# FFN chunks of a post-norm layer: z ahead of the transposes of h1, the second silu ahead of the norm's products, the centring behind the second norm's product

## What is computed

```python
# _L0_attn_ref: 12 layers of attention without a softmax, all linear in x but for q.k.v
for i in range(12):
    q, k, v = split(x @ Wqkv[i].T + bqkv[i])          # 16 heads of 8 channels
    att = einsum('bhqd,bhkd->bhqk', q, k) * scale
    y = einsum('bhqk,bhkd->bhqd', att, v)
    x = y @ Wproj[i].T + bproj[i] + x
x = layernorm(x_in + attention(x_in))                  # h1 below
gate, up = h1 @ w_gate.T / 127, h1 @ w_up.T / 127      # 384 hidden channels
x = layernorm(h1 + (silu(gate) * up) @ w_down.T / 127)
```

## Time and profile before

| what | us |
|---|---|
| median of 3 runs (lowest, highest) | 336.1 (335.86, 336.31) |
| the profiled execution, in all | 335.32 |
| its span | 333.5 |
| granted clock of PE over the span | 0.999 |
| PE busy | 317.8 (95% of the span) |
| DVE busy | 226.4 (68%) |
| ACT busy | 183.0 (55%) |
| POOL busy | 96.6 (29%) |

### The profile page before, as it was taken

One profiled execution on the slowest core, in us unless ns is written; L12 is line 12 of the kernel. 1 busy time (PEld: TensorE's weight loads), 2 busy tenths in 40 slices (PEclk: granted clock), 3 DMA queues, 4 the chain that ended last, 5 costly groups with the idle time before them and its releaser, 6 DMA issues.

```text
span 333.5 us, 8348 instructions
## 1 busy us (share of the span) xinstructions
PE 317.8 (95%) x3336; PEld 288.9 (87%) x3336; DVE 226.4 (68%) x638; ACT 183.0 (55%) x417; POOL 96.6 (29%) x89
## 2 busy tenths in 40 slices
PE   8899999999999999999999999999999999999993
PEld 7879889798897998979979799797997988888873
DVE  1167676775775757757677576676765569998974
ACT  3338757376483774846738467385572164444550
POOL 2006046050320502305023050140505034555533
PEclk9999999999999999999999999999999999999999
DMA  8751001010010200102002010020000000111112
GB/s 232 267 220 61 4 2 61 2 63 2 2 61 3 63 0 3 63 0 63 2 2 62 2 52 12 2 62 2 2 3 2 0 1 0 31 48 46 33 34 67
DMA packets 10660, 13.66 MB, mean 41 GB/s; under 512 B 512, under 2 KB 8832, under 8 KB 10496
## 3 DMA queue, kind: packets, MB, share of 16 engines
q1 hardware_dynamic: 8368, 11.94, 11.4%
q10 hardware_dynamic: 2256, 1.21, 1.3%
HBM read 11.04 MB, written 2.10 MB: 39 GB/s over the span
## 4 chain that ended last, share of the span: by engine, by line
PE 80%; DVE 9%; issue 3%; DMA 3%; ACT 2%; POOL 1%; ACTq 0%; POOLq 0%; DVEq 0%
PE ps L797 14%; PE ps L850 13%; PE ps L885 13%; PE ps L748 6%; PE ps L746 6%; PE ps L747 6%; PE ps L964 3%; PE ps L806 3%; PE ps L836 3%; DMA xt<-x_tok 3%; DVE s_rows L581 3%; PE ps L813 2%; DVE xt L681 2%; DVE mt L574 2%; PE ps L953 1%
## 5 line engine op out<-in xcount | busy, mean ns | idle before, releaser
L346 POOL TENSOR_TENSOR step_lo<-step,step_hi 128x512 fp32r<-128x512 f32 x44 | 54.9, 1279 | 180.3 <-ACT step_hi L430 180.3
L746 PE MATMUL ps<-state_hi,step_hi 128*128 128x258 f32 x176 | 50.7, 288 | 0.0
L850 PE MATMUL ps<-s_rows,w 32*128 32x256 f32 x768 | 44.8, 380 | 5.5 <-DVE s_rows L581 5.5
L748 PE MATMUL ps<-state_hi,step_lo 128*128 128x258 f32 x176 | 49.9, 283 | 0.0
L747 PE MATMUL ps<-state_lo,step_hi 128*128 128x258 f32 x176 | 49.6, 282 | 0.0
L850 PEld LDWEIGHTS ps<-s_rows,w 32*128 32x128 f32 x768 | 40.4, 185 | 7.4 <-ACT s_rows L424 7.4
L430 ACT CAST step_hi<-step 128x512 fp32r<-128x512 f32 x44 | 27.0, 619 | 33.8 <-DVE step L586 33.8
L797 PE MATMUL ps<-w,gram 128*128 128x128 f32 x352 | 44.0, 278 | 0.0
L797 PEld LDWEIGHTS ps<-w,gram 128*128 128x128 f32 x352 | 41.1, 192 | 1.0
L885 PE MATMUL ps<-step,gram 128*128 128x128 f32 x320 | 40.6, 281 | 0.0
L885 PEld LDWEIGHTS ps<-step,gram 128*128 128x128 f32 x320 | 37.3, 192 | 3.3 <-DVE step L586 3.3
(11 more groups left out here) (103 smaller groups left out, 502.7 us busy)
## 6 DMA issues: line engine op xcount, KB each, us to landing
w<-weights SPq DMA_DIRECT2D x12, 496.5 KB, 3.5
xchan<-x_chan SPq DMA_DIRECT2D x1, 2048.0 KB, 10.6
out<-xchan SPq DMA_DIRECT2D x7, 256.0 KB, 2.4
xt<-x_tok ACTq DMA_DIRECT2D x4, 256.0 KB, 7.5
xt<-x_tok SPq DMA_DIRECT2D x4, 256.0 KB, 5.3
fw_int<-ffn_weights SPq DMA_DIRECT2D x1, 576.0 KB, 4.8
out<-xchan SPq DMA_DIRECT2D x2, 128.0 KB, 2.4
cst<-consts ACTq DMA_DIRECT2D x1, 154.5 KB, 4.4
```

The source lines that it names most:

```text
L346: nc.gpsimd.tensor_tensor(group(step_lo, g), group(step, g), group(step_hi_f, g), ALU.subtract).then_inc(step_lo_ready, 1)
L746: nc.tensor.matmul(dst, l_hi, r_hi, start=True, stop=False)
L748: return nc.tensor.matmul(dst, l_lo, r_hi, start=False, stop=True)
L850: last = nc.tensor.matmul(n_banks(h)[:, k, :], w[r, s, WQ + P * i:WQ + P * (i + 1)], s_rows[r, h, i, :], start=i == 0, stop=i == QUADS - 1)
```

## The change

On POOL, norm2 of chunk c now comes ahead of the centring of chunk c+3. On ACT, the second silu of chunk c comes ahead of the norm products of chunk c+1. On DVE, z_part of chunk c+2 comes ahead of ht_part of chunk c+1. On PE, z of chunk c+2, with its wait, comes ahead of the transposes of chunk c+1. No instruction is added or taken away, and the steps ahead of the loops and behind them stay.

```diff
@@ POOL, chunk(c, slot, ahead) @@
                 if ahead >= 2:
                     pool.wait_ge(h1_ready, (c + 1) * CT + CT)
                     rstd1_part(c + 2)
+                if ahead > 0:
+                    norm2(c)
                 if ahead >= 3:
                     pool.wait_ge(z_done, c + 2)
                     centre(c + 3, 1 - slot)
-                if ahead > 0:
-                    norm2(c)
@@ ACT, chunk(c, slot, last) @@
                 gate(c, 0)
+                gate(c, 1)
                 if not last:
                     norm1(c + 1, 1 - slot)
-                gate(c, 1)
                 gate(c, 2)
@@ DVE, chunk(c, slot, ahead) @@
                 for j in range(HC):
                     hid_part(c, j)
+                if ahead >= 2:
+                    z_part(c + 2, c + 2, slot)
                 if ahead >= 1:
                     ht_part(c + 1)
                 if ahead >= 2:
-                    z_part(c + 2, c + 2, slot)
                     dve.wait_ge(rstd1_ready, c + 2)
                     var1_part(c + 2, slot)
@@ PE, chunk(c, slot, low, ahead) @@
                 for j in range(HC):
                     gate_stage(c, j, low)
-                if ahead >= 1:
-                    ht_stage(c + 1, 1 - slot)
                 if ahead >= 2:
                     pe.wait_ge(z_ready, c + 2)
                     z_stage(c + 2, c + 2, slot)
+                if ahead >= 1:
+                    ht_stage(c + 1, 1 - slot)
                 down_stage(c, last_chunk=ahead == 0)
```

## The result

The changed kernel takes 352.75 us (median of 4 runs, 352.12 to 353.95) against 336.18 before: a ratio of 1.0499, 95% interval 1.0467 to 1.0531. It is slower, as forecast, by more than forecast: 16.6 us in place of 10.7, and outside the range of 345.2 to 349.8. The profiled execution took 352.3 us with a span of 350.5, 17.0 above that of before, at a mean granted clock of 0.985.

What follows compares the result with a forecast made beforehand. The prediction took a chain of waits through down products, y, squares and hid as the bound. It added 10.3 us for five turns and 0.45 for the ACT edit, 10.75, to 336.1: 346.8 us, range 345.2 to 349.8.

Steps and rivals of the forecast that it cites:

- What bounds the kernel: In the FFN, a chain of waits rather than one engine's busy share; one turn per chunk, five turns 36.71 us.
- The stalled square: On DVE after y, one square takes 1.12 us beside POOL's centring, not 0.29; a stall of 0.83 us a turn.
- the ring: Chain from down products to y, squares, hid and down products again, with POOL and ACT steps between; forecast 9.40 us a turn.
- the next limit: In chunk 6, ACT: hid waits 0.22 us for the second silu, queued behind the four norm products.
- Centring behind the product, z waits: POOL's centring follows norm2's product, so PE waits some 2.75 us for z in five turns: 10.3 us more.
- Steps 1 to 5: From y to power, product, centring, its end and z's first product: 1.95, 1.21, 1.00, 1.04 and 0.15 us.
- step 2: POOL's second norm, power to product: 1.21 us in the loop, taken; 1.09 outside it.
- Step 6: On PE, z 0.89, transposes 0.44, down products 2.69, then 0.03 to y: 4.05 us a turn.
- z ahead on DVE: z_part before ht_part could become a second limit: 4.07 to 4.21 against PE's 4.05 us; taken as 0 a turn.
- ACT edit: Second silu ahead of the norm products: hidden in five turns, 0.45 us more for chunks 0 and 6 together.
- the fallen clock: Rival: PE's clock falls to 1.2 GHz in the new wait; 366.9 us, or 356.9 if half; chance 0.05.
- The first rival: The stall goes and PE does not wait, if xc is ready for z: turns of 7.0, 334.8 us; chance 0.03.

Runs made afterwards that it cites:

- e5: The kernel before with one edit, the centring of chunk c+3 moved to the start of POOL's pass c, ahead of both powers: 333.45 us.
- e1: The changed kernel with the centring put back ahead of norm2 on POOL, the PE, DVE and ACT edits kept: 336.43 us.
- e8: The changed kernel with the last up product of chunks 1 to 5 computed six times over, same result, to keep PE busy: 346.94 us.
- e6: The kernel before with the ACT edit alone, the second silu ahead of the norm products: 337.2 us.
- e4: The changed kernel with the centring of chunk c+3 moved to the start of POOL's pass c, the other three edits kept: 334.67 us.

## Why the prediction was wrong, step by step

- **What bounds the kernel**: right. The stalled square was on the ring: without it, and without a wait for xc, five turns take 34.06 (e5) in place of 36.71. What it called the next limit, ACT, is not the next one in these turns: in e5 that is PE's own work.
- **Centring behind the product, z waits**: right in mechanism and place, and e1 shows that without it nothing is lost. Steps 1 to 5 were within 0.02: 1.95, 1.20, 1.00, 1.04 and 0.15 between the starts at 279.06, 281.01, 282.21 and 283.21 and z's at 284.40. z starts 5.34 after y, forecast 5.35. The stop shows as 2.57 where 2.75 was forecast, as the forecast counted from the start that a next gate product would have had, 0.17 before the last one's end (281.43 and 0.40). In the fifth turn, whose pass is outside POOL's loop, step 2 took the 1.09 that the prediction had read there and not used.
- **Step 6, mis-sized**: 4.05 forecast, 4.31 measured in turn 3 (306.88 to y at 311.19, from 1.15, 0.44, 2.69 and 0.03). The 0.89 for z was its length on a chain that runs on from the end of the product before; behind a stop it has to be counted from its first start, which the 1.06 of the earlier trace rows already showed, and the first product behind a stop takes 0.37 in place of 0.28, which adds another 0.09. With it a turn is 9.64 in place of 9.40, and five turns at full clock are 48.09 (e8) in place of 47.0.
- **z ahead on DVE**: right. y is released by the down products in every turn, after 0.32 to 1.45 us of idle time on DVE.
- **ACT edit**: right, and near its size in the changed kernel, 0.15 in chunk 0 and 0.22 in chunk 6 for the forecast 0.45 together; on its own it costs more (e6), by the late transposes, which I hadn't followed up.
- **The failed step: the fallen clock at a chance of 0.05**, outside the range. The mechanism and its place were those of that rival, as e8 shows: 5.8 us less with PE busy, at 346.94 well inside the range even with step 6 at its true size. It came in three turns of five in the profile, 1.4 to 1.65 each, between the forecast's none and the rival's 2 to 4 in all five. I let a row with a stop of 0.99 speak for stops of 2.75, which no row showed. Such a step has two ends, and the upper one belonged in the range: five falls of even half the 4.02 would have put it at 356.9. The Trainium skill's rule (TensorE: Matmul & The Clock Gate, Part 1), that the lower clock is the default and activity lifts it, is borne out here: 0.50 behind the stop, 1.00 again while the products still run.
- **The first rival's time**: its condition was false in the changed kernel. In e4, which meets it, 334.67 stands beside the 334.8 worked out for it.

With the clock kept up, e8 took 346.94 beside the forecast 346.8. That closeness is luck: its profiled execution, 347.45, is 12.1 above that of before where 10.75 was forecast. Of the 1.4 between them, 1.1 is step 6, and 0.4 lies ahead of the first gate product (272.01 against 271.63), which no edited step precedes; chunks 0 and 6 took 0.1 less than forecast.

## What to carry to other kernels

A step that is moved behind another on its own queue inherits everything that the other waits for: before moving it, ask which pass of its consumer reads it, and if the new place is later than that, move the whole step one pass ahead instead, where the order is the same and the wait is gone. Where an edit opens a stop on TensorE that is longer than any in the trace, price what comes behind it at both clock levels and keep both ends in the range. And a chain's stage that starts behind a stop is longer than the same stage in a running chain by the latency of its first product.

## What the runs showed of the hardware

- The granted clock fell to 0.50 behind stops of PE of 2.1 to 2.57 us, in some turns and not in others of the same length, and each fall cost 1.4 to 1.65 us on the ring. In one turn of the changed kernel it came only 0.6 us or more after the products had started again; in the other two z ran slow from its first product on. I had given this a chance of 0.05; in the profiles with filler, whose stops were 1.6 us or less, no fall was seen.
- Ten needless products in each of five chunks made a kernel 5.8 us faster.
- The first product of z behind a stop takes 0.37 us in place of 0.28, behind one of 0.24 us (e8) as behind one of 2.57.
- One centring on POOL, over 128x512, stalls a square on DVE for as long as it runs (1.12 to 1.17 us in place of 0.29), but a hid step, which reads one of its inputs from PSUM, not at all (0.69 us in e4, from 282.48, with POOL's product running from 281.94 to 282.98). The Trainium skill (SBUF — State Buffer, SBUF: two separate sides) states a lock that GpSimd, where it starts first, holds for a whole instruction against DVE steps with two inputs in SBUF, as the squares are; the lengths agree.
